# Rows of the first attention tiles gathered in the preparation, another order of the attention's steps, and the clearing of a table moved to feed-forward

## The reference

```python
q = (x @ qW + qb).reshape(N, H, D)          # N = 50000, H = 8, D = 16
k = (x @ kW + kb).reshape(N, H, D)
v = (x @ vW + vb).reshape(N, H, D)
scores = sum(q[src] * k[dst], -1) / sqrt(D) + edge_attr @ eW + eb
ex = exp(scores - segment_max(scores, dst)[dst])
attn = ex / maximum(segment_sum(ex, dst), 1e-8)[dst]
out = segment_sum(v[src] * attn[:, :, None], dst).reshape(N, 128) @ oW + ob
x = layer_norm(x + out); h = gelu(layer_norm(x @ f1W + f1b)) @ f2W + f2b
x = layer_norm(x + h)
```

## Time and profile before

| | us |
|---|---|
| three runs: lowest, median, highest | 5865.55, 5870.03, 5874.11 |
| profiled execution: its own time | 5857.95 |
| its span | 5856.1 |
| preparation (0 to 109.65) | 109.65 |
| attention (109.65 to 756.55) | 646.90 |
| feed-forward (756.55 to about 1690) | 933 |
| everything behind | 4166 |

### The profile page before, as it was taken

How to read it: one execution, slowest core, us unless ns; L and a number is a source line. 1 busy time by engine, 2 the same in 40 slices (tenths; PEclk the granted TensorE clock), 3 DMA queues, 4 the chain that set the end, 5 groups by cost and what they waited for, 6 DMA issues and landing times. The chain is left out here.

```text
span 5856.1 us, 75382 instructions
## 1 busy us (share of the span) xinstructions
PE 4174.1 (71%) x16190; PEld 2478.6 (42%) x16190; DVE 3930.2 (67%) x13570; ACT 2803.5 (48%) x6338; POOL 3499.8 (60%) x3137
## 2 busy tenths in 40 slices
PE   5666659999995555465664779967996679656654
PEld 2333335555542333244443445534443334356543
DVE  6577759999995444376674875557666888746533
ACT  0344438787871100266663445534444555446543
POOL 4677668888867888455555650056105758855455
PEclk8777869999997777688886999989998999878876
DMA  6233333333323344466664774467445667657521
GB/s 219 70 85 82 77 79 110 114 110 114 110 85 75 62 62 63 66 192 185 189 191 138 205 210 132 128 187 216 151 142 161 188 171 213 189 182 222 175 81 54
DMA packets 785242, 802.39 MB, mean 137 GB/s; under 512 B 138080, under 2 KB 551848, under 8 KB 784666
## 3 DMA queue, kind: packets, MB, share of 16 engines
q1 hardware_dynamic: 403802, 393.43, 23.1%
q0 software_dynamic: 117504, 209.42, 15.0%
q10 hardware_dynamic: 263488, 194.72, 10.1%
HBM read 445.32 MB, written 351.92 MB: 136 GB/s over the span
## 5 line engine op out<-in xcount | busy, mean ns | idle before, releaser
L476 PE MATMUL gate_bank<-gate_ht,gate_whh 128*128 128x512 f32 x1764 | 882.5, 615 | 65.8 <-DVE gate_n L546 36.9
L944 POOL DMA_INDIRECT xh<-mean_xh,mean_pos_all x392 | 378.1, 965 | 359.5 <-DVE mean_xh L1046 134.1
L476 PEld LDWEIGHTS gate_bank<-gate_ht,gate_whh 128*128 128x128 f32 x1764 | 325.2, 196 | 468.5 <-issue 371.4
L2082 PE MATMUL back_ps_sums<-back_same,back_rows 128*128 128x512 f32 x400 | 288.8, 888 | 289.1 <-DMA back_rows<-x_a,back_idx 289.1
L1465 POOL DMA_INDIRECT ffn_rows<-att_sums,ffn_idx x392 | 393.9, 1005 | 124.0 <-issue 108.2
L291 POOL DMA_INDIRECT gate_rows<-h_a,by_pos x200 | 199.0, 995 | 431.6 <-POOLq L118 326.5
L472 PE MATMUL gate_bank<-by_rank,gate_win 128*128 128x512 f32 x882 | 435.1, 593 | 1.8 <-DVE by_rank L355 1.8
L612 ACT ACTIVATE gate_n<-gate_n,gate_b_ih 128x512 f32<-128x512 f32 x294 | 212.1, 721 | 400.4 <-issue 255.4
L1517 PE MATMUL ffn_ps_f<-ffn_hg,ffn_f 128*128 128x512 f32 x784 | 389.1, 597 | 3.4 <-ACT ffn_hg L1700 3.2
L1510 PE MATMUL ffn_ps_u<-ffn_xs_t,ffn_up_w 128*128 128x512 f32 x784 | 386.7, 595 | 1.1 <-issue 1.1
L2063 POOL DMA_INDIRECT back<-back_out,back_dest x200 | 324.3, 1622 | 70.5 <-issue 62.8
(11 more groups left out here) (270 smaller groups left out, 11633.1 us busy)
## 6 DMA issues: line engine op xcount, KB each, us to landing
mean_x<-x_a SPq DMA_DIRECT2D x196, 256.0 KB
back<-blank ACTq DMA_DIRECT2D x99, 264.0 KB, 4.5
mean_rows<-back SPq DMA_DIRECT2D x98, 264.0 KB
hp<-mean_xh SPq DMA_DIRECT2D x98, 264.0 KB
gate_x<-xh SPq DMA_DIRECT2D x98, 264.0 KB
gate_hot<-hot_rows SPq DMA_DIRECT2D x100, 256.0 KB
ffn_x<-in_x_in SPq DMA_DIRECT2D x98, 256.0 KB
ffn_xr<-in_x_in SPq DMA_DIRECT2D x98, 256.0 KB
```

The source lines that it names most:

```text
L476: last = nc.tensor.matmul(bank_[:, :], whh[:, c * D:(c + 1) * D], ht[:, t.slot4, :], start=not inputs, stop=True)
L944: nc.gpsimd.indirect_dma_start(out=g["xh"][:, :], out_offset=bass.IndirectOffsetOnAxis(ap=pos_all[:, t.n, j:j + 1], axis=0), in_=xh[:, t.n ...
L2082: last = nc.tensor.matmul(ps_sums[t.slot][:, :], rows[:, t.slot4, j, :], same[:, t.slot, j, :], start=j == 0, stop=j == J - 1)
```

## The change

- *A store of gathered rows.* The class `AttentionFeed` lives over both preparation and attention. It holds twelve slots of rows in place of four. SP loads one list with the indices of all 50 tiles as its first transfer in the preparation (the host lays out `edge_blocks` for that), and the attention's eleven weights there too. GpSimd issues the 64 gathers of tiles 0 to 7 in the preparation; in the attention it gathers tile n when tile n-12 has been turned.
- *The attention's order.* DVE's product of q and k moves from step +1 to +2, the product with v and the two scans behind it from +3 to +4; ACT's score copy from +2 to +3, logarithm and inverse from +4 to +5, the copy of the turned rows from +0 to +1, all three groups to the head of its step. PE's step begins with the output product of tile -6, and its transposes stand ahead of the head sums. A tile is still stored in step n+7.
- *The histogram.* The high one-hots of columns 1 and 2 of four are made by ACT: square of (digit - high), then ReLU(1 - square) over the pair. DVE keeps columns 0 and 3 and all the low ones; GpSimd makes none.
- *The table `back`* is cleared by SP in feed-forward, one transfer of 264 KB a tile, and one at the end. The transfer of zeros into `sums` is gone with the table.

```diff
+class AttentionFeed:
+    SLOTS, AHEAD, LOADS = 12, 8, 11
...
+        self.idx = sb("idx", [P, ET, J, 2], I32)
+        self.send, self.recv = (sb(n, [P, self.SLOTS, J, D]) for n in ("send", "recv"))
...
+    def load_lists(self, sp):
+        sp.dma_start(self.idx[:, :, :, :].rearrange("p s j c -> p (s j c)"), self.g["edge_blocks"]
+                     ).then_inc(self.idx_loaded, 16)
...
+    def gather(self, n):
+        slot = n % self.SLOTS
+        for j in range(J):
+            for col, rows, sem in ((1, self.send, self.sent), (0, self.recv, self.received)):
+                self.nc.gpsimd.indirect_dma_start(
+                    out=rows[:, slot, j, :], out_offset=None, in_=self.g["x_in"][:, :],
+                    in_offset=bass.IndirectOffsetOnAxis(ap=self.idx[:, n, j, col:col + 1], axis=0)
+                ).then_inc(sem[slot], 16)
...
         @block.sync
         def _(sp):
-            for dst_, src_ in ((qw[:, :], g["qW"]), (kw[:, :], g["kW"]), (vw[:, :], g["vW"]), (ow[:, :], g["oW"]),
...
-                sp.dma_start(dst_, src_, allow_slow_non_contiguous=True).then_inc(w_loaded, 16)
             def step(tile_at):
-                if t := tile_at(0):
-                    wait_alone(sp, sent[t.slot4], 64 * t.u4)
-                    wait_alone(sp, received[t.slot4], 64 * t.u4)
-                    sp.dma_start(idx[:, t.slot4, :, :].rearrange("p j c -> p (j c)"),
-                                 g["edge_blocks"][t.n]).then_inc(idx_loaded[t.slot4], 16)
...
         @block.gpsimd
         def _(pool):
-            def step(tile_at):
-                if t := tile_at(0):
-                    wait(pool, idx_loaded[t.slot4], 16 * (t.u4 + 1))
-                    wait(pool, rows_turned, t.n - 1)
-                    pool.nop(nofuse=True)
-                    for j in range(J):
-                        for col, rows, sem in ((1, send, sent), (0, recv, received)):
-                            nc.gpsimd.indirect_dma_start(
-                                out=rows[:, t.slot4, j, :], out_offset=None, in_=g["x_in"][:, :],
-                                in_offset=bass.IndirectOffsetOnAxis(ap=idx[:, t.slot4, j, col:col + 1], axis=0)).then_inc(sem[t.slot4], 16)
-            over_tiles(pool, ET, 0, step)
+            for n in range(feed.AHEAD, ET):
+                wait(pool, rows_turned, n + 1 - slots)
+                pool.nop(nofuse=True)
+                feed.gather(n)
...
         @block.tensor
         def _(pe):
...
             def step(tile_at):
+                if t := tile_at(6):
+                    wait(pe, att_done, t.n + 1)
+                    wait(pe, out_done, t.n)
+                    for j in range(J):
...
+                    last.then_inc(out_made, 1)
                 if t := tile_at(1):
...
+                if t := tile_at(0):
+                    wait(pe, sent[t.n % slots], 64 * (t.n // slots + 1))
...
+                    last.then_inc(rows_turned, 1)
                 if t := tile_at(2):
...
                                      edge_t[:, t.slot4, :], start=False, stop=True).then_inc(s_made, 1)
-                if t := tile_at(0):
...
-                    last.then_inc(rows_turned, 1)
-                if t := tile_at(6):
...
-                    last.then_inc(out_made, 1)
             over_tiles(pe, ET, 6, step)
...
@@ -1241,6 +1268,31 @@
             nc.vector.tensor_copy(eb[:, :], ps_s[:, 0:1]).then_inc(eb_done, 1)
             def step(tile_at):
+                if t := tile_at(2):
+                    wait(dve, k_made, t.n + 1)
...
+                if t := tile_at(4):
...
+                    nc.vector.tensor_tensor(pv[:, t.slot, :], v[:, t.slot4, :], ex[:, t.slot, 0, :],
...
                                                    ALU.min, ALU.mult).then_inc(att_done, 1)
-                if t := tile_at(3):
...
-                    nc.vector.tensor_tensor(pv[:, t.slot, :], v[:, t.slot4, :], ex[:, t.slot, 0, :],
-                                            ALU.mult).then_inc(pv_done, 1)
...
@@ -1314,19 +1341,28 @@
             def step(tile_at):
                 if t := tile_at(1):
+                    wait(act, rows_turned, t.n + 1)
+                    wait(act, v_made, t.n - 1)
+                    nc.scalar.activation(send_t[:, t.slot, :], ps_send[:, :], ACT.Copy).then_inc(send_done, 1)
+                    nc.scalar.activation(recv_t[:, t.slot, :], ps_recv[:, :], ACT.Copy).then_inc(recv_done, 1)
+                if t := tile_at(3):
+                    wait(act, s_made, t.n + 1)
+                    wait(act, arg0_done, t.n - 1)
+                    nc.scalar.activation(s[:, t.slot, :], ps_s[:, :], ACT.Identity, bias=eb[:, :]).then_inc(s_done, 1)
+                if t := tile_at(5):
+                    wait(act, den_done, t.n + 1)
+                    wait(act, inv_done, t.n - 1)
+                    nc.scalar.activation(log[:, t.slot, :], den[:, t.slot, :], ACT.Ln).then_inc(log_done, 1)
+                    wait(act, log_done, t.n + 1)
+                    wait(act, att_done, t.n - 1)
+                    nc.scalar.activation(inv[:, t.slot, :], log[:, t.slot, :], ACT.Exp, scale=-1.0).then_inc(inv_done, 1)
+                if t := tile_at(1):
...
-                if t := tile_at(4):
...
-                    nc.scalar.activation(log[:, t.slot, :], den[:, t.slot, :], ACT.Ln).then_inc(log_done, 1)
...
-                if t := tile_at(2):
...
-                    nc.scalar.activation(s[:, t.slot, :], ps_s[:, :], ACT.Identity, bias=eb[:, :]).then_inc(s_done, 1)
-                if t := tile_at(0):
...
-                    nc.scalar.activation(send_t[:, t.slot, :], ps_send[:, :], ACT.Copy).then_inc(send_done, 1)
-                    nc.scalar.activation(recv_t[:, t.slot, :], ps_recv[:, :], ACT.Copy).then_inc(recv_done, 1)
...
+            def clear_back(n):
+                sp.dma_start(g["back"][n * SUPER:(n + 1) * SUPER, :].rearrange("(p j) d -> p (j d)", j=J),
+                             g["blank"][:, :]).then_inc(g["back_blank"], 16)
...
                     sp.dma_start(flat(xr[:, t.slot, :, :]), nm_tile(g["x_in"], t)).then_inc(xr_loaded[t.slot], 16)
+                    clear_back(t.n)
             over_tiles(sp, NT, 8, step)
+            clear_back(NT)
...
+    def high_hots_act(self, act, group, digits, one):
+        scalar = self.nc.scalar
+        first, pair = 4 * group + 1, self.apart[:, group % 2, :, :]
+        wait(act, self.high_done_act, group - 1)
+        for k in range(2):
+            last = scalar.activation(pair[:, k, :], digits[:, 0:2 * self.rows], ACT.Square,
+                                     bias=self.high_less[:, first + k:first + k + 1])
+        last.then_inc(self.apart_done, 1)
+        wait(act, self.counted, first + 2 - self.HOT_BUFFERS)
+        act.wait_ge(self.apart_done, group + 1)
+        b = first % self.HOT_BUFFERS
+        scalar.activation(self.hot_high[:, b:b + 2, :].rearrange("p b n -> p (b n)"),
+                          pair.rearrange("p b n -> p (b n)"), ACT.Relu,
+                          bias=one[:, 0:1], scale=-1.0).then_inc(self.high_done_act, 1)
...
     def count_column(self, pe, c):
         b = c % self.HOT_BUFFERS
-        if c % 4:
-            pe.wait_ge(self.high_done, c - c // 4)
+        if c % 4 in (1, 2):
+            pe.wait_ge(self.high_done_act, c // 4 + 1)
         else:
-            pe.wait_ge(self.high_done_pool, c // 4 + 1)
+            pe.wait_ge(self.high_done, 2 * (c // 4) + 1 + (c % 4) // 3)
...
         @block.sync
         def _(sp):
+            feed.load_lists(sp)
...
             sp.dma_start(ob[:, :], on_all(g["ob"])).then_inc(consts_loaded, 16)
+            feed.load_weights(sp)
...
         @block.scalar
         def _(act):
-            act.wait_ge(zeros_set, 2)
-            act.dma_start(g["sums"][EP:EP + SUPER, :].rearrange("(p j) d -> p j d", j=J), zeros[:, :, :]
-                          ).then_inc(filled, 16)
-            for t in range(NT + 1):
-                act.dma_start(g["back"][t * SUPER:(t + 1) * SUPER, :].rearrange("(p j) d -> p (j d)", j=J),
-                              g["blank"][:, :]).then_inc(g["back_blank"], 16)
-            act.wait_ge(filled, 16)
+            act.wait_ge(ones_set, 1)
+            act.wait_ge(digits_done, 1)
+            act.wait_ge(nodes.split_done, 3)
+            for group in range(ECOLS // 4):
+                nodes.high_hots_act(act, group, digits, ones)
         @block.gpsimd
         def _(pool):
-            pool.wait_ge(digits_done, 1)
-            pool.wait_ge(nodes.split_done, 2)
-            for c in range(0, ECOLS, 4):
-                nodes.high_hot(pool, nc.gpsimd, c, digits, nodes.high_done_pool)
+            pool.wait_ge(feed.idx_loaded, 16)
+            for n in range(feed.AHEAD):
+                feed.gather(n)
...
             for c in range(ECOLS):
                 nodes.low_hot(dve, vector, c, digits)
-                if c % 4:
+                if c % 4 in (0, 3):
                     nodes.high_hot(dve, vector, c, digits, nodes.high_done)
...
```

(5 more changed lines are left out.)

155 lines of the change are left out of this document (79 added, 76 removed).

## The result

The changed kernel takes 5891.35 us (median of six runs, 5884.25 to 5898.54), the kernel before 5868.01 beside it: 1.0048 times, with an interval of 1.0032 to 1.0065. Forecast were 5726 and 0.85 for faster. It is 23 us slower.

The account below looks back on a forecast made before the run. GpSimd's gathers were taken to bound attention. Preparation 100, first gather 0.6, gathers 455.6, drain 46.4 put feed-forward's start at 602.6 instead of 756.55: -154, ten given back, -144; 5870 - 144 = 5726 us, range 5690 to 5862.

Parts of the forecast that it names:

- Preparation, the histogram beside the gathers: Preparation: histogram takes 65 us (bounds 57 to 75), gathers finish by 91, stage ends at 100 instead of 109.65.
- Rival C: Preparation: GpSimd issues no gather while DVE's short bf16 operations run, shifting everything by 47 us, to 5773; chance 0.10.
- with eight tiles in store PE and DVE can run ahead: Attention: PE and DVE run ahead until about tile 33, at 8.26 us a step against GpSimd's 10.85.
- the ten given back: Attention: 10 us conceded for late signals near the store's end and in the drain, turning -154 into -144.
- rival B: Attention: PE's late results cost every tile what they cost now; -29 us, whole 5841; chance 0.13.
- ACT's copy ten us after a matmul's recorded end: Attention: score matmul ends at 422.27, copied at 432.66; maybe a late matmul, the sum taken as unaffected.
- Rival D: Attention: PE at its low clock sets the pace, 13.2 us a tile with late signals; +50 us, 5920; chance 0.08.
- 336 gathers: Attention: the gathers left for this stage take 336 x 1.356 = 455.6 us if PE keeps within twelve tiles.
- the drain: Attention's end: last gather's end to feed-forward's first instruction stays 46.4 us, bounds 38 to 55.
- the first gather: Attention's start: first gather comes 0.6 us after the preparation's end at 100.
- ACT's group: Preparation: ACT's two squares and one ReLU take 1.13 us per four columns, plus a wait of 0.1.
- the clear: Feed-forward: SP's one extra clearing transfer a tile costs 0 us, bound above 72.

Follow-up runs that it names:

- e13: Changed kernel with PE signalling the histogram's columns every fourth column, by 4, instead of one by one; 5857.0 us against the kernel before's 5842.6.
- e11: Changed kernel with the 99 clearing transfers issued by SP in the preparation and none in feed-forward; 5351.6 us against the kernel before's 5453.0.
- e3: Changed kernel with 256 straight loads by SP replacing the early gathers, tile n gathered when n-4 is turned; 5378.8 us against the kernel before's 5453.7.
- e16: The same edit of the changed kernel as e3, run on another chip; 5756.1 us against the kernel before's 5830.6.

## Why the prediction was wrong

*Preparation, the histogram beside the gathers.* This step failed, and it decided the sign. I bounded the gather by the histogram and the histogram by the gather, both through DVE: 57 to 75 us for the histogram. On the first kind it ran from 15 to 154 (to 83 on the second), since PE, which the step did not price at all, needed up to 2.7 us a matmul (e13). In place of -10 the preparation brought +65. None of the bounds held it: even the upper, a gather slowed to 2.3, was about GpSimd, and GpSimd was not slowed (64 gathers in 80 us, 1.256 from start to start, the lower bound). Rival C had GpSimd starve beside DVE, after the Trainium skill's rule (SBUF — State Buffer, "SBUF: two separate sides"). The second kind does not show this: with DVE busy 56.73 of the 60 us from 20 to 80, on one-hots of 0.29 and 0.31 us, 48 gathers are issued, as many as on the first kind, where DVE is busy 4.73, and half of the first 64 take 0.947 or less. Whether these one-hots run in the modes that the rule is about, no run here shows.

*Attention, "with eight tiles in store PE and DVE can run ahead".* On the first kind this failed too: -21 for the stage in place of -134 (502.6 and the ten given back, for 646.9). From the first gather to the last it went at 492.1 / 42 = 11.72 a tile, hardly under the 11.85 of before, and all 50 tiles took 625.8, 12.5 each, where the kernel before needs 639 from its first gather on, 12.8. That is rival B's pace. B spoke of late results at an unchanged rate of the work; what it was is a lost rate, and it grows with the length of the run, so the store, which was to bridge it, made the runs longer (56 gathers at the start, where the longest run of the kernel before is 33). The earlier trace rows was the row that showed it: ACT's copy ten us after a matmul's recorded end. I wrote that it might be a late matmul and that the sum was the same under either reading. It was not: a late signal can be bridged by a store, matmuls that come through more slowly than GpSimd gathers cannot. That the end in the row is computed (the Trainium skill, Perfetto Trace Analysis, the section on the Tensor Engine instruction) agrees with e13, where PE's rows show matmuls of 0.27 to 0.45 us in a stretch in which four columns, eight matmuls, took 22.

*Rival D* had the sign and the engine, PE, but not the cause. Its granted clock does fall to 0.52 in the hold-up (20 to 80 us); by the earlier trace rows that makes a pair of matmuls 1.92 us long in place of 1.08, while a column went from 0.34 us to 5.4. (Its 1.83 us hold eight transposes and the four matmuls of the output: the output is one part of the twelve, not a further one. The sum stays.)

*What held, on the second kind.* 336 gathers took 459 (104.4 to 563.4; 455.6 forecast), the drain 45.5 (46.4), the first gather came 0.7 behind the preparation's end (0.6), the preparation ended at 103.8 (100; ACT's group takes 1.41 where I had 1.23, its two squares 0.79 together and its ReLU 0.62 where I had 0.64 and 0.49), the clear cost nothing (e11). Feed-forward then starts at 609, forecast 602.6 and, with the ten given back for late signals, 612.6. No late signals came; that the ten cover these misses is luck. The gain is 97 and not 144, since before is 52.6 us faster in its attention there: the gaps to be won were those of the first kind alone.

So the sum was made from a trace of the one kind with a behaviour of PE that only the other has: gaps and late copies were counted as a gain to be had, and as cause was taken the supply of tiles.

## What to carry to other kernels

Results that others see long after a matmul's recorded end are a lost rate of PE until shown otherwise: count how many come through in a stretch, and what runs beside it, before a deeper buffer is counted on. Every stage into which work is moved has to be priced on all engines there, and also on the one that neither touches the work nor shares a port with it. A kernel that overlaps long runs of indirect gathers with matmuls should be timed on more than one chip; a limit of four tiles in place of twelve went with 29 us more attention on the second kind (e3) and with 31 to 45 us less on the first (e16, against e13 and the changed kernel; single runs on different chips).
